# Weighted sums of the attentions in three parts, between the transposes of the next unit, and output transposes read by ScalarE

## The reference

```
L0x: softmax(mask(q k^T) / sqrt(128)) v, heads joined, @ W_out.T + b_out
L2x: a = softmax(q1 k1^T * s) - lambda * softmax(q2 k2^T * s);  o = a v, heads joined
     o = o * rsqrt(mean(o*o) + eps) * norm_w;  o @ proj_w.T + proj_b
L3x: o = softmax(rope(q) rope(k)^T * s + bias) v;  att = o @ Wout.T + b_out
     gate = sigmoid(att @ Wgate.T + b_gate);  gate * att + (1 - gate) * residual
x = x + attention(layernorm(x));  x = x + ffn(layernorm(x))
```

## Time and profile before

| | |
|---|---|
| runs | 1288.03, 1301.16, 1305.8 us; median 1301.16 |
| the profiled execution | 1308.73 us, its span 1306.9 us |
| busy share of the span | PE 82%, PE weight loads 75%, DVE 51%, ACT 39%, POOL 30% |
| granted PE clock over the span | 0.814 of 2.4 GHz |

### The profile page before, as it was taken

One profiled execution on the slowest core, in us unless ns is written; L12 is line 12 of the kernel. 1 busy time (PEld: TensorE's weight loads), 2 busy tenths in 40 slices (PEclk: granted clock), 3 DMA queues, 4 the chain that ended last, 5 costly groups with the idle time before them and its releaser, 6 DMA issues. The chain is left out here.

```text
span 1306.9 us, 19893 instructions
## 1 busy us (share of the span) xinstructions
PE 1077.4 (82%) x7374; PEld 976.3 (75%) x7374; DVE 670.0 (51%) x1808; ACT 513.0 (39%) x987; POOL 397.4 (30%) x396
## 2 busy tenths in 40 slices
PE   3899999999988999889989762989169987359992
PEld 2888889999977899768888662888148877358882
DVE  7788511111257343667778643343567655444443
ACT  1443434444433334444444321655224323045552
POOL 4333300010013002300010054446634335545552
PEclk9866589999995899968788765999667656579996
DMA  9999800000000000000000013654200000155553
GB/s 324 170 172 170 156 1 1 1 1 1 1 1 1 1 1 1 1 1 1 1 1 2 1 33 115 177 172 147 65 1 1 1 1 20 36 168 174 174 165 97
DMA packets 70574, 83.52 MB, mean 64 GB/s; under 512 B 5297, under 2 KB 57528, under 8 KB 70352
## 3 DMA queue, kind: packets, MB, share of 16 engines
q1 hardware_dynamic: 64336, 71.71, 24.1%
q0 software_dynamic: 4992, 8.45, 1.9%
q10 hardware_dynamic: 1152, 2.10, 0.4%
HBM read 51.88 MB, written 32.18 MB: 64 GB/s over the span
## 5 line engine op out<-in xcount | busy, mean ns | idle before, releaser
L2167 ACT ACTIVATE hT<-PS,par 128x512 f32<-128x512 f32 x200 | 137.3, 689 | 186.4 <-PE PS L2115 184.9
L2207 DVE SCALAR_TENSOR_TENSOR X<-PS,wts,X 128x128 f32<-128x128 f32 x272 | 76.6, 344 | 231.5 <-PE PS L2127 231.5
L837 PEld LDWEIGHTS PS<-vblk,hT 128*128 128x128 f32 (+1 forms) x1152 | 175.1, 239 | 0.0
L1050 ACT ACTIVATE hT<-PS 128x512 f32<-128x512 f32 (+1 forms) x192 | 91.4, 490 | 205.0 <-PE PS L820 195.3
L837 PE MATMUL PS<-vblk,hT 128*128 128x27 f32 (+2 forms) x1152 | 170.3, 301 | 0.0
L820 PE MATMUL PS<-par,score 128*128 128x128 f32 (+1 forms) x640 | 135.8, 365 | 15.3 <-ACT score L1030 8.1
L820 PEld LDWEIGHTS PS<-par,score 128*128 128x128 f32 (+1 forms) x640 | 106.4, 190 | 25.2 <-issue 13.9
L2127 PEld LDWEIGHTS PS<-regA,hT 128*128 128x128 f32 x1024 | 119.2, 192 | 2.8
L2127 PE MATMUL PS<-regA,hT 128*128 128x128 f32 x1024 | 119.5, 275 | 0.0
L1097 POOL TENSOR_TENSOR score<-score,mx 128x1232 f32<-128x1232 f32 x32 | 72.0, 2249 | 121.7 <-DVE mx L922 121.7
L1878 PE MATMUL PS<-q_up,halves 128*112 128x256 f32 (+1 forms) x276 | 87.9, 318 | 16.1 <-DVE hT L1990 8.8
(11 more groups left out here) (301 smaller groups left out, 2108.9 us busy)
## 6 DMA issues: line engine op xcount, KB each, us to landing
regA<-L3f_w SPq DMA_DIRECT2D x23, 704.0 KB
regB<-L2f_w SPq DMA_DIRECT2D x23, 578.0 KB
L2f_sorted_x<-empty_row SPq DMA_DIRECT2D x8, 1161.0 KB, 21.9
L3f_sorted_x<-empty_row SPq DMA_DIRECT2D x8, 1161.0 KB, 22.1
regA<-L0f_w SPq DMA_DIRECT2D x4, 768.0 KB, 15.9
regA<-L2f_sorted_x SPq DMA_DIRECT2D x23, 129.0 KB, 3.7
regB<-L3f_sorted_x SPq DMA_DIRECT2D x23, 129.0 KB, 4.0
par<-params SPq DMA_DIRECT2D x1, 2386.0 KB, 12.2
```

The costliest lines, as they stand in the source:

```text
L837: last = nc.tensor.matmul(PS[:, 6, h0 * VW:(h0 + nh) * VW], pT, vblk[0:w, b, 3 * j * VW:(3 * j + nh) * VW], start=False, stop=j == NBLK - 1)
L1050: nc.scalar.activation(hT[:, u % 2, i, 0:full], PS[:, bank, 0:full], ACT.Copy)\
L2167: nc.scalar.activation(hT[:, n % 2, k, :], PS[:, i % 4, :], c["act"], bias=pc(f"{tag}_b1")[:, col:col + 1]).then_inc(h_ready.sem, 1)
```

## The change

- `weighted` gets a part i of the three groups. The parts of unit u-1 are put between the transposes of unit u: transposes 0, sums 0, transposes 1, `out_project`, sums 1, router rows, transposes 2, sums 2, router logits and ranks, gate. Before, `weighted(u)` stood whole at the end of iteration u.
- `lag` is 3, in L3x 2. `normalise(u-1)` stands in iteration u. The router's statistics start one iteration later, and so do the powers that POOL makes for them; the scatters of L3x are dealt out otherwise (3, 3 in the last two tiles' iterations, then 3, 3, 4, where it was 2, 2, 2, then 3, 3, 4).
- ACT reads the output transposes (`evacuate_oT`) ahead of a unit's first group, and in L3x the transposed projection (`evacuate_attT`) after the exponentials. The exponentials of unit u+1 stand after the first group of unit u, not after the third.
- In L0x and L2x the bias goes into `fin` in `finish`, and the sum to x is an instruction of its own: in L0x it is made an iteration later, between the two passes of `maxima` (`gate_out` of L3x too); in L2x right behind `finish`. `out_transpose` waits for `att_ready` (the bias was added) and no longer for the sum to x.

```diff
-            lag = 1 if tag == "L3x" else 2
+            lag = 2 if tag == "L3x" else 3
...
-                def weighted(u):
+                def weighted(u, i):
                     b = tile_of(u) // TG
-                    if u:
+                    if i == 0 and u:
                         pe.wait_ge(o_used.sem, o_used.at(u))
-                    if tag == "L3x" and u >= 2:
+                    if i == 0 and tag == "L3x" and u >= 2:
                         pe.wait_ge(g_in.sem, g_in.at(u - 1))
-                    for j, (h0, nh, w) in enumerate(BLOCKS):
-                        if j % 4 == 0:
-                            pe.wait_ge(pT_ready.sem, pT_ready.at(3 * u + j // 4 + 1))
+                    pe.wait_ge(pT_ready.sem, pT_ready.at(3 * u + i + 1))
+                    for j in groups[i]:
+                        h0, nh, w = BLOCKS[j]
...
                 def out_transpose(t):
                     pe.wait_ge(o_ready.sem, o_ready.at(t + 1))
                     if t:
-                        free = aT_ready if tag == "L3x" else x_done
-                        pe.wait_ge(free.sem, free.at(t))
+                        pe.wait_ge(att_ready.sem, att_ready.at(t))
...
                     if 0 < u < units:
-                        transposes(u, (0, 1))
+                        transposes(u, (0,))
+                    if 0 < u <= units:
+                        weighted(u - 1, 0)
+                    if 0 < u < units:
+                        transposes(u, (1,))
                     if done is not None:
                         out_project(done)
+                    if 0 < u <= units:
+                        weighted(u - 1, 1)
...
                     if 0 < u < units:
                         transposes(u, (2,))
+                    if 0 < u <= units:
+                        weighted(u - 1, 2)
...
-                    if u < units:
-                        weighted(u)
...
-                def evacuate_oT(t):
-                    v.wait_ge(oT_psum.sem, oT_psum.at(t + 1))
...
                 def finish(t):
                     v.wait_ge(y_psum.sem, y_psum.at(t + 1))
...
+                    att = gdiff[:, t % 2, :] if tag == "L3x" else fin[:, 2 + t % 2, :]
+                    nc.vector.tensor_tensor(att, PS[:, 7, P:2 * P], pc(f"{tag}_bo"), ALU.add).then_inc(att_ready.sem, 1)
+
+                def add_attended(t):
+                    v.wait_ge(att_ready.sem, att_ready.at(t + 1))
+                    nc.vector.tensor_tensor(X[:, t, :], X[:, t, :], fin[:, 2 + t % 2, :], ALU.add).then_inc(x_done.sem, 1)
...
                     if u + 2 < units:
-                        maxima(u + 2)
+                        maxima(u + 2, add_to_x)
...
-                    if u < units:
-                        normalise(u)
+                    if 0 < u <= units:
+                        normalise(u - 1)
...
+                def evacuate_oT(t):
+                    a.wait_ge(oT_psum.sem, oT_psum.at(t + 1))
+                    nc.scalar.activation(ocT[:, t % 2, :], PS[:, 7, 0:P], ACT.Copy if tag != "L2x" else ACT.Identity,
+                                         scale=pc("L2x_norm") if tag == "L2x" else 1.0).then_inc(oT_ready.sem, 1)
...
+                    if done is not None:
+                        evacuate_oT(done)
                     if u < units:
...
+                        evacuate_pT(u, 0)
                     if u + 1 < units:
                         exps(u + 1)
+                    if tag == "L3x" and done is not None:
+                        evacuate_attT(done)
+                    if u < units:
+                        evacuate_pT(u, 1)
...
+                        evacuate_pT(u, 2)
...
-            stats_unit = {"L2f": 9, "L3f": 5}[tag]
+            stats_unit = {"L2f": 10, "L3f": 6}[tag]
```

More of the change, by code:

```diff
@@ L900, in vector, with maxima @@
             def vector(v, st):
-                def maxima(u):
+                def maxima(u, between=None):
                     t = tile_of(u)
@@ new lines, in evacuate_pT @@
+                def evacuate_pT(u, i):
+                    n, width = 3 * u + i, len(groups[i]) * P
+                    bank = bank_of(("exps", n))
+                    a.wait_ge(pT_psum.sem, pT_psum.at(n + 1))
+                    if i == 0 and u >= 2:
+                        a.wait_ge(o_psum.sem, o_psum.at(u - 1))
+                    full = width if groups[i][-1] < NBLK - 1 else width - P
+                    nc.scalar.activation(hT[:, u % 2, i, 0:full], PS[:, bank, 0:full], ACT.Copy)\
+                        .then_inc(*((pT_ready.sem, 1) if full == width else (a_step, st.one())))
+                    if full < width:
+                        rows = BLOCKS[-1][2]
+                        nc.scalar.activation(hT[0:rows, u % 2, i, full:width], PS[0:rows, bank, full:width],
+                                             ACT.Copy).then_inc(pT_ready.sem, 1)
@@ L1033, in scalar @@
                 exps(0)
                 for u in range(units + lag + (tag == "L3x")):
-                    if tag == "L3x" and u >= 2:
-                        t = u - 2
+                    done = after_unit(u) if u < units + lag else None
+                    if tag == "L3x" and u > lag:
+                        t = u - lag - 1
                         a.wait_ge(g_in.sem, g_in.at(t + 1))
                         nc.scalar.activation(gin[:, t % 2, :], gin[:, t % 2, :], ACT.Tanh, scale=0.5).then_inc(g_tanh.sem, 1)
-                    g = route["logits_group"](u) if route else None
+                    if done is not None:
+                        evacuate_oT(done)
@@ L1040, in scalar @@
                     if u < units:
[L1041 to L1048, removed]
-                            full = width if blocks[-1] < NBLK - 1 else width - P
-                            nc.scalar.activation(hT[:, u % 2, i, 0:full], PS[:, bank, 0:full], ACT.Copy)\
-                                .then_inc(*((pT_ready.sem, 1) if full == width else (a_step, st.one())))
-                            if full < width:
-                                rows = BLOCKS[-1][2]
-                                nc.scalar.activation(hT[0:rows, u % 2, i, full:width], PS[0:rows, bank, full:width],
-                                                     ACT.Copy).then_inc(pT_ready.sem, 1)
+                        evacuate_pT(u, 0)
@@ L1106, in pool @@
                         shift(t)
-                        if tag == "L3x" and t >= 3:
-                            less_xn(p, t - 3)
-                    g, left = divmod(t - 6, TG)
-                    if tag == "L0x" and left == 0 and 0 <= g < NG - 1:
+                        if tag == "L3x" and t >= 4:
+                            less_xn(p, t - 4)
+                    g, left = divmod(t - 9, TG)
+                    if tag == "L0x" and left == 0 and 0 <= g < NG - 2:
                         after_nm["pool_group"](p, g)
@@ L1121, in pool @@
                         route["pool_tile"](p, st, t)
+                if tag == "L0x":
+                    after_nm["pool_group"](p, NG - 2)
                 if tag == "L3x":
-                    for t in range(NT - 3, NT):
+                    for t in range(NT - 4, NT):
                         less_xn(p, t)
@@ L1641, in pool_tile @@
             def pool_tile(p, st, t):
[L1642 removed]
+                g, left = divmod(t - (8 if tag == "L3f" else 3), TG)
                 if left == 0 and 0 <= g < late:
```

68 lines of the change are left out of this document (36 added, 32 removed).

## The result

The changed kernel is slower: 1379.74 us in the median of four runs (1371.89 to 1383.51) where the kernel before has 1297.27 (1288.03 to 1305.8). The ratio is 1.063 (95% interval 1.058 to 1.068). Medians are of all runs; the ratios leave out the executions that lie over 1.5% above the fastest of their kernel. That is Rival B of the prediction, TensorE that doesn't get back to 2.4 GHz, and not the forecast.

What follows compares the result with a forecast made beforehand. PE was taken as the bound, its larger loss being time at 1.2 GHz. 20 + 13 + 5 - 1 = 37 us off the profiled 1308.7 gave 1272, as median 1264 (1243 to 1285); whole range 1212 to 1345.

Steps and rivals of the forecast that it cites:

- Rival B: In the three attentions PE doesn't get back to 2.4 GHz: +77 us, 1378 us (1340 with half the units); chance 0.23.
- What the new order of the work itself does to the clock: In the three attentions, the new order's own effect on PE's clock: taken as 0, called the largest unknown.
- Rival A: PE keeps 2.4 GHz after three units in each of the three attentions: -94 us, so 1207 us; chance 0.22.
- Idle that goes: PE's waits removed in L0x, L2x and L3x, four items together: 20 us, between 13 and 24.
- L978's 6.3: In L0x, PE's five waits at L847 for the sum to x go: 6.3 us, between 5 and 6.3.
- the third group's 3.1: In L2x, the third transpose group's waits for ACT's read of the first go: 3.1 us.
- the router's waits in L2x: Waits of router transposes (4.3 us) and logits (1.7) in L2x go; with L3x's 1.3, 7.3 us.
- the projection's 6.6 in L3x: In L3x the projection's 6.6 us wait for DVE's read of the output transpose: half goes, 3.3 (0 to 6.6).
- Idle that stays: L847's waits stay: 10.9 us for L957 in L2x, 6.8 for `normalise` in L3x; three tails cost 1 us (0 to 4).
- The wait that is added: `weighted(u-1, 0)` waits for DVE's `normalise(u-2)` behind fewer transposes: between 0 and 16 us, taken as 0.
- Edits that I cost at nothing: ACT's reads, moved exponentials, POOL's powers and scatters: taken as 0; 13 us if ACT's cover were gone.
- The clock after stalls: Fewer stalls mean less time at 1.2 GHz: 13 us for three router stalls in L2x, 5 for five L0x waits.

Runs made afterwards that it cites:

- e1: Changed kernel with the weighted sums of unit u-1 whole at the end of PE's iteration: 1290.8 us, 0.991 of the kernel before.
- e3: Changed kernel with the weighted sums of unit u-1 whole between the second and third transpose groups: 1252.79 us, 0.964 of the kernel before.
- e4: Changed kernel plus one block of 24 unused transposes in each attention, at unit 4: 1372.83 us, 1.053 of the kernel before.
- e5: Changed kernel with 34 zero columns added to each thin matmul of the weighted sums: 1228.38 us, 0.942 of the kernel before.
- e9: Changed kernel with 10 zero columns added to each thin matmul of the weighted sums: 1322.16 us.
- e12: Changed kernel with 22 zero columns added to each thin matmul of the weighted sums: 1254.67 us, 0.970 of the kernel before.
- e8: e5 with DVE's `normalise` ahead of the norm's statistics and apply in L0x: 1229.41 us, 0.949 of the kernel before.
- e11: Changed kernel with DVE reading the output transposes again, ahead of its maxima: 1384.94 us, 1.070 of the kernel before.
- e7: e3 with 34 zero columns added to each thin matmul, as in e5: 1223.68 us, 0.945 of the kernel before.
- e6: Kernel before, order unchanged, with 34 zero columns added to each thin matmul: 1284.87 us, 0.990 of the kernel before.

## Why the prediction was wrong

**The step that failed** is the one on the clock: "What the new order of the work itself does to the clock no row shows; I take 0". It isn't 0, it is the largest term: +91 us of PE's busy time with the same matmuls. e1 and e3 show that the order of the sums alone sets it, e4 that its units in L0x and L2x neither raise the clock nor regain it, and e5, e9 and e12 that the width of L839's matmuls decides whether it comes up. The prediction had the row for it: the 4.3 us before the rise without a thin matmul, and its length in the new order, computed as 2.6 us and now measured as 2.68. I gave that 0.23 because it was one rise among several. It was the only argument I had that says how the clock comes up, and Rival A by its own words had none. Two readings beside it were off. All 11 transposes stood in the 4.3 us, not 10, and with them 16 other matmuls (12 for scores, two each of L852 and L835), which is more than a few. And 2.6 us isn't the longest run of the new order: the gate and the router make longer ones, and the three rises among its sums (818.7, 1074.7 and 1125.9 us) stand at their ends. The 56% of L0x at 1.2 GHz is 63% with the start of the stage counted (0.68).

**Rival B's working.** Its sum was 1378 us, the median 1379.7, and that is closer than the parts deserve. A unit with output takes 7.97 us in L2x (priced at 8.1). In the prediction's own stretches, first sum to last, L0x took 119.5 us (126 priced), L2x 253.3 (257) and L3x 135.6 (143, and it had two rises), so +60 and not +77. The rest of the 82 is, but for 3 us outside the stretches, the place of the profiled executions: before's lies 11.5 us above its median, after's 7.9 below. Against the profiles the change costs 63 us, against the medians 82.

**"Idle that goes", 20 us.** It went: -21.6 in the cuts, and the items are gone one by one, L978's 6.3, the third group's 3.1, the router's waits in L2x, and most of the projection's 6.6 in L3x, of which half was priced. In the prediction's own stretches, which start with the first sum, it is 43.4 to 15.5; 6 us of that only moved ahead of their start. (The ends of the terms as given add up to 15 to 23, not 13 to 24.) But this doesn't show that the order hides it. At 1.2 GHz PE takes 8.0 us for a unit with output instead of 4.6 (e4, from 617.44 to 622.03), and the engines it waits for have that much more time. Where the clock is up again the idle comes back in other places: 63.3 us in e1, 58.4 in e3, 68.1 in e5. I priced a wait as if its removal were kept; here the next engine (DVE, busy for 144 of 180 us of L2x in e5) takes most of it.

**"Idle that stays".** L849's longest wait for `root_mean_square` is 5.3 us (5.7 before), and 9.8 in total for 10.9; its waits for `normalise` in L3x (L951) are 7.4 us for 6.8: right.

**"The wait that is added", taken as 0 within 0 to 16.** 0.4 us at 1.2 GHz, 7.9 in L0x at the full clock in e5. Both inside the range; e8 shows that it is a place at which DVE's lateness surfaces, not a cost of its own.

**"Edits that I cost at nothing".** Right for ACT's reads at 1.2 GHz (e11). The moved exponentials, statistics and scatters were not run one by one; all of the change without its order, gains and costs together, gives 0.991 (e1).

**The clock after stalls, 13 + 5 us.** Not tested as such, so both terms stay estimates. e1, which lacks the waits for the sum to x, has its L0x at 112.5 us for 118.6: 6 us won where the terms for L0x give 6.3 + 5, and of these 4.9 are busy time and 1.2 idle.

**The Trainium skill** was weighed twice. By "TensorE: Matmul & The Clock Gate", section "Part 4: PE-mode transpose", PE-mode transposes don't count as busy for the clock as matmuls do. e4 disagrees for the kernel's `transpose`, which the trace lists as a MATMUL: the clock rose during the block of 24 in L0x (73.9) and in L2x (613.2), where the changed kernel has no rise near. By the section on depth-cycling, idle between groups of matmuls makes the clock swing; here less idle came with less clock. Falls next to waits speak for it, as at 626.9 in e4 (0.53 us); but before's falls at 78.8 and 99.3 us have no wait over 0.12 us in the 5 us ahead. The same page's section "HAM oscillation — how this bites in real kernels" advises, for a matmul with few rows, a loop order without waits or more rows by padding, so that the clock stays up; its reason is idle time on DMAs. Padding, here of columns, paid as well (e5), but not by that reason: the stretch that stayed at 1.2 GHz is 96% busy.

## What to carry to other kernels

Before you interleave a run of wide matmuls or transposes with thin ones, look up where the granted clock rises and what PE did just before; if the new order leaves no such run, price each unit at 1.2 GHz as a case of its own and give it weight. Read busy time beside the matmul count: busy time that grows at an equal count is the clock, however good the waits look, and waits measured at the low clock say little on those at the high one. Where a matmul and its weights' load take as long with few columns as with many (0.21 us a pair with 27 and with 128 columns at 1.2 GHz), columns of zeros are nearly free and can be worth more than a reordering: here 151 us in the changed kernel, and versions (e5 and e7) 5.5 to 5.8% faster than the kernel before. It is no rule: the same columns gave 1% in the order before (e6).

## What the runs showed that I had not expected

TensorE 96% busy for 242 us (232.0 of 242.4) at 1.2 GHz throughout, while L2x before, with more idle (189.7 of 216.0), reached 0.75. The median of the changed kernel falls steadily as its thin matmuls go from 27 to 37, 49 and 61 columns: by 58, 67 and 26 us. And a stretch at the start of a trace without a clock record is printed as 1.00: by its durations the whole first attention of the changed kernel, of e9 and of e11 ran at 1.2 GHz, and so did TensorE's work in the first 36 to 66 us of every other profiled run.

What stays open: what makes the clock fall. In e5 each of the eleven falls in its cuts has a wait of PE of 0.8 to 5.8 us just ahead of it or across it, but no run took those waits away alone, and in the kernel before some falls have none. Open too is why the clock needs what it needs to rise: the runs show that order and width of the thin sums decide it, not by what rule.
